# Second cross attention with its rounded projections in whole 16-bit numbers, output by token tile; peaks of the second self attention turned first

## What is computed

```python
def _qdq(x):
    s = jnp.maximum(jnp.max(jnp.abs(x), axis=-1, keepdims=True) / 127.0, 1e-08)
    return jnp.clip(jnp.round(x / s), -127.0, 127.0) * s
q = _qdq(x) @ _qdq(wq).T + bq
kv = cond @ wkv.T + bkv
k, v = jnp.split(kv, 2, axis=-1)
attn = jax.nn.softmax(jnp.einsum('bnhd,bmhd->bhnm', q, k) * scale, axis=-1)
o = jnp.einsum('bhnm,bmhd->bnhd', attn, v).reshape(B, N, C)
out = _qdq(o) @ _qdq(wp).T + bp
```

## Time and profile before

| | before |
|---|---|
| median of 3 runs | 1515.16 us |
| lowest and highest | 1513.21 and 1516.91 us |
| profiled execution, whole time | 1516.96 us |
| its span in the trace | 1515.1 us |
| TensorE busy, mean granted clock | 93%, 0.957 |
| VectorE, ScalarE, GpSimd busy | 66%, 52%, 5% |

### The profile page before, as it was taken

The page is one execution under the profiler, slowest core; times in us unless marked ns, Lnnn a source line. Parts: engine busy times, 40 slices in busy tenths (PEclk is TensorE's granted clock), DMA queues, the critical chain, the costliest instruction groups (busy, mean ns, idle before and its releaser), DMA issues. The chain is left out here.

```text
span 1515.1 us, 31884 instructions
## 1 busy us (share of the span) xinstructions
PE 1415.0 (93%) x11772; PEld 1087.6 (72%) x11772; DVE 999.5 (66%) x1651; ACT 783.7 (52%) x1130; POOL 78.4 (5%) x71
## 2 busy tenths in 40 slices
PE   6999999999979989999989999969999688899998
PEld 4677776777735479999977877846666365799997
DVE  6666677666645467666538777768999333676664
ACT  3677777777741545554422222327887103555552
POOL 0000000000010300000011121110000100000000
PEclk9999999999989979999999999978999769899999
DMA  5333443333223077656115233237785120676662
GB/s 167 73 89 86 121 104 85 83 83 89 49 76 141 1 244 264 206 197 209 37 47 168 106 126 109 84 87 164 170 175 116 49 53 9 207 254 211 213 216 75
DMA packets 133457, 190.94 MB, mean 126 GB/s; under 512 B 74972, under 2 KB 96702, under 8 KB 130175
## 3 DMA queue, kind: packets, MB, share of 16 engines
q1 hardware_dynamic: 133391, 190.04, 43.6%
HBM read 153.86 MB, written 17.48 MB: 113 GB/s over the span
## 5 line engine op out<-in xcount | busy, mean ns | idle before, releaser
L187 PE MATMUL psum<-m_x_hi,m_gu_hi 128*128 128x256 f32 x780 | 222.8, 286 | 3.2 <-DVE m_h L2381 2.9
L188 PE MATMUL psum<-m_x_hi,m_gu_lo 128*128 128x256 f32 x780 | 222.1, 285 | 0.0
L189 PE MATMUL psum<-m_x_lo,m_gu_hi 128*128 128x256 f32 x780 | 222.0, 285 | 0.0
L1527 DVE TENSOR_REDUCE x_peaks<-psum 128x2048 f32 (+1 forms) x64 | 146.4, 2291 | 51.6 <-PE psum L1419 51.6
L187 PE MATMUL psum<-x_w_hi,x_ctx_hi 128*128 128x256 f32 x512 | 159.0, 311 | 0.0
L187 PEld LDWEIGHTS psum<-m_x_hi,m_gu_hi 128*128 128x128 f32 x780 | 150.7, 193 | 6.9 <-DVE m_h L2381 3.3
L188 PEld LDWEIGHTS psum<-m_x_hi,m_gu_lo 128*128 128x128 f32 x780 | 150.7, 193 | 1.5
L189 PEld LDWEIGHTS psum<-m_x_lo,m_gu_hi 128*128 128x128 f32 x780 | 150.5, 193 | 0.0
L188 PE MATMUL psum<-x_w_hi,x_ctx_lo 128*128 128x256 f32 x512 | 145.1, 283 | 0.0
L189 PE MATMUL psum<-x_w_lo,x_ctx_hi 128*128 128x256 f32 x512 | 144.9, 283 | 0.0
L1657 DVE TENSOR_TENSOR e_wqp<-e_wqp,x_probs 128x1024 f32<-128x1024 f32 x124 | 141.7, 1220 | 3.1 <-ACT x_probs L1672 2.8
(11 more groups left out here) (310 smaller groups left out, 2777.9 us busy)
## 6 DMA issues: line engine op xcount, KB each, us to landing
m_gu_raw<-in_m_gu SPq DMA_DIRECT2D x41, 768.0 KB, 4.3
e_w<-x_keys_dram SPq DMA_DIRECT2D x45, 512.0 KB, 6.9
m_gu_raw<-in_m_gu SPq DMA_DIRECT2D x18, 1024.0 KB, 5.0
x_ctx_raw<-in_ctxT SPq DMA_DIRECT2D x64, 256.0 KB, 2.7
m_dn_raw<-in_m_down SPq DMA_DIRECT2D x16, 768.0 KB, 4.3
m_dn_raw<-in_m_down SPq DMA_DIRECT2D x18, 512.0 KB, 5.1
x_keys_dram<-x_keys_hi SPq DMA_DIRECT2D x16, 512.0 KB, 3.2
x_keys_dram<-e_wqp SPq DMA_DIRECT2D x16, 512.0 KB, 2.6
```

What stands on the lines that cost most here:

```text
L187: pe.matmul(out, a[0], b[0], start=start, stop=False, skip_group_check=True)
L188: pe.matmul(out, a[1], b[0], start=False, stop=False, skip_group_check=True)
L189: return pe.matmul(out, a[0], b[1], start=False, stop=stop, skip_group_check=True)
L1527: dve.tensor_reduce(peaks[:, t, 4 * m:4 * m + 4, bass.ds(k, 1)].rearrange("p h k -> p (h k)"), g.psum[:, at:at + BANKS, :], AX, ALU.max).t ...
```

## The change

- `grid_step` no longer multiplies by the step size in its last step. It writes the whole numbers (up to 127 in magnitude) to a tensor given as `whole`. `wqT`, `wpT`, the rounded x (`x16`) and the rounded output (`o16`) become 16-bit floats. The step sizes of the weights are kept in `g.x1_grid`.
- Query: ScalarE spreads the step size of each token over 128 columns, TensorE turns it into a row for all partitions (bank 3), and ScalarE copies that (`x_row`) before its half of x. VectorE then scales the product (`scalar_tensor_tensor`), and adds the bias in a further instruction.
- `c3`: ScalarE spreads the step sizes of wp (four instructions), TensorE turns them after the peaks, ScalarE copies them (`wp_row`), and only then fills its row of ones.
- `c4`: SyncE loads `bp` and `bv` (256 KB each) ahead of its loop; GpSimd adds `bp` to x in two instructions. The sums are no longer rotated.
- `c5`: the reciprocals are taken of the sums as they stand in PSUM, 512 per partition and tile, and outputs are divided straight from PSUM before they are turned. Each token tile goes alone through bias, rounding, turning, copy and product; then it is scaled and added. The product with one row of ones is gone.
- `stage_attn1`: the peaks are turned ahead of the values' product; `tops(0)` waits for the first half of the queries alone.

```diff
@@ grid_step
-            dve.tensor_scalar(tiles[i], tiles[i], ROUND, col(grid, i), ALU.subtract, ALU.mult).then_inc(done, 1)
+            dve.tensor_scalar(whole[i], tiles[i], ROUND, None, ALU.subtract).then_inc(done, 1)
@@ stage_cross1
-        wpT = sb("wpT", [P, NC, D], F32)
-        wqT = sb("wqT", [P, NC, D], F32)
+        wpT = sb("wpT", [P, NC, D], F16)
+        wqT = sb("wqT", [P, NC, D], F16)
@@ query on TensorE
-                        pe.wait_ge(x_rounded, 1)
+                        pe.wait_ge(x_spread_ready, NT)
+                        for t in range(NT):
+                            last = pe.transpose(g.bank[3][:, t * P:(t + 1) * P], x_spread[:, t, :], g.ident[:, :])
+                        last.then_inc(x_row_turned, 1)
+                        pe.wait_ge(grid_done, NT * GRID_STEPS[-1])
...
+                            if m == 2:
+                                pe.wait_ge(x_row_taken, 1)
@@ query on ScalarE
+                    act.wait_ge(grid_done, 2 * NT)
+                    for t in range(NT):
+                        act.activation(x_spread[:, t, :], g.zeros[:, 0:P], ACT.Identity,
+                                       bias=grid[:, t:t + 1]).then_inc(x_spread_ready, 1)
...
+                            act.wait_ge(x_row_turned, 1)
+                            act.activation(x_row[:, :], g.bank[3][:, 0:L], ACT.Copy).then_inc(x_row_taken, 1)
@@ query on VectorE
                         for m in range(NC):
+                            dve.scalar_tensor_tensor(out=qT[:, m, :],
+                                                     in0=g.bank[2 + m // 2][:, (m % 2) * L:(m % 2 + 1) * L],
+                                                     scalar=g.x1_grid[:, 0, m:m + 1], in1=x_row[:, :], op0=ALU.mult,
+                                                     op1=ALU.mult).then_inc(q_ready, 1)
+                        for m in range(NC):
+                            dve.tensor_scalar(qT[:, m, :], qT[:, m, :], bias[:, 0, m:m + 1], Y_HD ** -0.5, ALU.add,
+                                              ALU.mult).then_inc(q_ready, 1)
@@ c3 on ScalarE
+                    for m in range(NC):
+                        act.activation(wp_spread[:, m, :], g.zeros[:, 0:P], ACT.Identity,
+                                       bias=g.x1_grid[:, 1, m:m + 1]).then_inc(wp_spread_ready, 1)
+                    act.wait_ge(wp_row_turned, 1)
+                    act.activation(wp_row[:, :], g.bank[1][:, :], ACT.Copy)
@@ c4
+                    pool.wait_ge(bp_loaded, 16)
+                    for t in range(NT):
+                        pool.tensor_tensor(g.x[:, t, :], g.x[:, t, :], bp[:, :], ALU.add)
...
+                    sp.dma_start(bp[:, :], A["x1_bp"]).then_inc(bp_loaded, 16)
+                    sp.dma_start(bv[:, :], A["x1_bv"]).then_inc(bv_loaded, 16)
@@ c5 on TensorE
+                    for t in range(NT):
+                        pe.wait_ge(divided, t + 1)
+                        for grp in range(4):
+                            last = pe.transpose(g.bank[t][:, grp * P:(grp + 1) * P], oT[:, t, grp // 2, grp % 2, :],
+                                                g.ident[:, :])
                         last.then_inc(turned, 1)
                     for t in range(NT):
+                        pe.wait_ge(step_done, GRID_STEPS[-1] * (t + 1))
                         for c in range(NC):
+                            last = pe.transpose(g.bank[2 + t].bitcast(F16)[:, c * P:(c + 1) * P],
+                                                o16[:, t, c * P:(c + 1) * P], g.ident16[:, :])
+                        last.then_inc(o_turned, 1)
+                        pe.wait_ge(o_taken, t + 1)
+                        for c in range(NC):
+                            last = pe.matmul(g.bank[6 + t][:, :], oqT[:, t, c * P:(c + 1) * P], wpT[:, c, :],
+                                             start=(c == 0), stop=(c == NC - 1))
+                        last.then_inc(projected, 1)
@@ c5 on VectorE
                     for t in range(NT):
+                        dve.reciprocal(inv[:, t, :, :, :], of_tile(6, t)).then_inc(inverted, 1)
                         dve.wait_ge(inverted, t + 1)
+                        dve.tensor_tensor(oT[:, t, :, :, :], of_tile(4, t), inv[:, t, :, :, :],
+                                          ALU.mult).then_inc(divided, 1)
                     dve.wait_ge(bv_loaded, 16)
                     for t in range(NT):
+                        dve.wait_ge(turned, t + 1)
+                        dve.tensor_tensor(o[:, t, :], g.bank[t][:, :], bv[:, :], ALU.add).then_inc(biased, 1)
+                        dve.wait_ge(biased, t + 1)
+                        for step in range(len(GRID_STEPS)):
+                            grid_step(dve, step, [o[:, t, :]], [o16[:, t, :]], grid[:, t:t + 1], per_grid[:, t:t + 1],
+                                      step_done, GRID_STEPS[-1] * t)
                     for t in range(NT):
                         dve.wait_ge(projected, t + 1)
+                        dve.scalar_tensor_tensor(out=y[:, t, :], in0=g.bank[6 + t][:, :], scalar=grid[:, t:t + 1],
+                                                 in1=wp_row[:, :], op0=ALU.mult, op1=ALU.mult).then_inc(scaled, 1)
+                        dve.wait_ge(scaled, t + 1)
+                        residual(dve, g, t, y[:, t, :])
@@ stage_attn1 on TensorE
-                pe.wait_ge(q_taken, 2)
                 for i in range(B_KV):
+                    if i < 2:
+                        pe.wait_ge(q_taken, i + 1)
                     if i == B_KV // 2:
                         pe.wait_ge(q_placed, 16 * J)
                     tops(i)
+                pe.wait_ge(tops_read, B_KV)
+                for t in range(NT):
+                    last = pe.transpose(g.bank[2][0:B_H, t * P:(t + 1) * P], peak[:, t, :], g.ident[:, :])
+                last.then_inc(peak_turned, 1)
                 pe.wait_ge(wv_loaded, 16)
-                pe.wait_ge(tops_read, B_KV - 1)
```

136 lines of the change are left out of this document (52 added, 84 removed).

## The result

The kernel after takes 1500.07 us (median of 4 runs, 1498.84 to 1501.55) against 1516.04 us of the kernel before beside it (4 runs, 1513.21 to 1518.34): a ratio of 0.990, 95% interval 0.9884 to 0.9916, so 16 us or 1% less. The prediction was 1501.2 us, range 1496.0 to 1508.0; its sum was 14.0 us. The profiled execution took 1501.55 us, its span 1499.7.

The account below looks back on a forecast made before the run. Bounds: TensorE up to and in the chunk loop, VectorE in the context-tile loop, a chain of waits in the output block. 4.9 + 7.8 + 2.5 - 1.2 = 14.0 us saved; 1515.16 - 14.0 = 1501.2 us, range 1496.0 to 1508.0.

Parts of the forecast that it names:

- Query: Query's product: 16 records instead of 32 save 5.3 us, the row copy costs 0.4; net 4.9 saved, passed on whole.
- the longer idle brings the clock to 0.50: Query, lower end of the gain: after some 2.5 us idle, product and part of the keys cost about 2 us more.
- Peaks' block: Before the context-tile loop: block ends about 0.9 us later, hidden by the second scores' wait for keys; counted 0, bounds 0 to 0.9.
- GpSimd's sums: Loop over context tiles: adding bp on GpSimd disturbs VectorE's gapless additions; 1.2 us lost, middle of 0 and 2.4.
- Port rival: Context-tile loop: both GpSimd sums each stop VectorE for 1.2 us, 1.2 more than counted; 1502.4 us; chance 0.20.
- Output block: End of second cross attention: a chain of waits, by token tile with 16-bit products, ends at 1194.9 instead of 1202.7; 7.8 us saved.
- Self attention: Second self attention: peaks turned first bring transfers earlier and perhaps a higher clock; 2.5 us saved, bounds 0.7 and 4.1.
- The transfer's part: Second self attention: peaks turned earlier let their DMAs land 1.2 us sooner; gain 0.7 to 1.2, taken as 1.0.
- The clock's part: Second self attention: without the pause before the first score the clock may be 2.4 GHz; at most 2.9 us, half taken, 1.5.
- Clock rival: Query's idle brings 1.2 GHz (1.9 us lost) and the self attention's clock stays low (1.7 less gained); 1504.8 us; chance 0.17.
- The rival that has the kernel slower: TensorE, nearly idle in the output block, stays at 1.2 GHz through the self attention; 19 us lost, 1521.7 us; chance 0.03.
- 16-bit no faster: Query and output products gain no speed from 16 bits: query loses 0.4 us, output block gains about 3; 1511.3 us; chance 0.06.

Follow-up runs that it names:

- e10: Kernel after with GpSimd's two sums moved to the start of the loop over chunks and ScalarE's row of ones filled first; 1500.62 us, ratio 0.9888.
- e15: Kernel after with the second cross attention's output product in fp32 instead of 16 bits; 1507.54 us, ratio 0.9933.
- e1: Kernel before with only the second self attention's edit (peaks turned ahead of the values' product); 1514.68 us, ratio 0.999.
- e13: Kernel after with e3, e10, the query's copies reordered, and needless products in TensorE's waits from query to self attention; 1490.32 us, ratio 0.9849.
- e11: Kernel after with three needless fp32 products ahead of the second self attention's search for peaks; 1494.80 us, ratio 0.9855.
- e3: Kernel after with outputs and sums copied and turned before dividing, as before, so 16 reciprocals per tile instead of 512; 1494.37 us, ratio 0.9842.

## Why the prediction was right

**The total: right, with errors that cancelled.** The parts gave 1.5 us less than predicted in the query and 0.7 less in the peaks' block, and 1.3 more in the loop over context tiles, 0.3 more in the output block and 1.3 more in the self attention. That they add up to 15.0 for 14.0 is in part luck.

**Query: right but for the clock.** 16 records by 0.12 gave 1.9 us; the rows show 1.92 at full clock. Row copy 0.4: the product began 0.27 later. Net gain 5.0 in six of the nine kernels that have the new query and no warm products there, against the predicted 4.9; in the profile of after it was 3.4, because of "the longer idle brings the clock to 0.50", which the step had as its lower end ("about 2 us more"; measured 1.6). VectorE and the loop over chunks passed the gain on, as the step said.

**Peaks' block: the delay was right, the cover held for a reason that wasn't worked out.** The delay was put at 0.9, and it was 0.7 to 1.0 in nine kernels. The step then hid it behind the DMA wait at 1024.25. The first group of scores and the first exponential come ahead of that wait, and they were late. VectorE's first addition was not; it came 16.8 us after the peaks' reduction, against 17.2 in before. The second group's keys had landed 9.8 us after the reduction instead of 10.7, so it no longer waited for them and began 0.4 sooner. By e10 the order on ScalarE costs 0.4 us there, within the step's 0 to 0.9.

**GpSimd's sums: the number was near, the path to it was not.** The step said that "anything that holds VectorE up there reaches the end", and took 1.2 as the middle between 0 and 2.4, without a mechanism. The runs show 2.2 us lost where the two engines meet, 1.2 made good in the rest of the row, and about 1 at the end. The reading behind it, a row "without a gap", was too coarse: 25 additions in 28.65 us have small pauses between them. The Port rival had the loss at the spot right (2.2 of its 2.4) and the time wrong. The loop's total in after (151.05 against 151.13) hides the 1 us, since its first addition came 1.1 us sooner after the first exponential.

**Output block: 8.1 for 7.8.** Reciprocals 3.36 (predicted 3.4), tile 0 rounded 13.5 us after the first sum (13.7), four products at 1.2 GHz 1.86 (1.7 to 2.0), end at 21.45 (21.8). The chain ended on VectorE and TensorE in turn, as drawn. What the sum left open, e15 settles: the 16 bits are 5.9 of it. Sum and measurement both count from the profile of before, 29.55; from e1's 27.94 the gain would be 6.5.

**Self attention: right on average, by two ends that don't average in a run.** The transfer's part, predicted 1.0, is 0.7 to 1.2 in all eight kernels. The clock's part is 2.9 or about nothing, kept in four of eight; "half" describes no run, but their mean (2.2 together) is near the 2.5. In the profile of after it was the whole: 3.8.

**The rivals.** The Clock rival was half true in the profile of after: its query half came (1.6), its self-attention half did not. The rival that has the kernel slower, with a clock that never rises in the self attention, did not come; it overlooked that the peaks' search runs at 1.2 GHz already in before and can only gain there. "16-bit no faster" is excluded by 1.92 and 1.02 us.

**What is open.** Why the clock falls in some profiles and not in others with the same idle time ahead (query 3 of 9; second score 4 of 8). Each kernel's timeline is read from one profiled execution, so how often each case comes in the timed runs isn't known. The two groups of e13's runs, 7 us apart and with different mean clocks, may be this; no trace of the slower group shows where. What the order by token tile is worth by itself is open too.

## What to carry to other kernels

A product in 16 bits pays its full difference where TensorE is the chain: 5.0 and 5.9 us here, and both follow nearly from record counts and one neighbouring row. After every edit that makes TensorE's work shorter, look for the waits that it makes longer. And where a stage full of TensorE work runs at clock 0.50 behind a pause of 1.7 us, try needless products in the pause: three of them, 1.3 us of work, brought 5.8 us up to the first score and 4.4 over the stage. Read a row of back-to-back work for its spacing, and not only for gaps: here 0.01 us an addition made good 1.2 us. And when a forecast takes the middle between two ends, ask whether the runs will lie at the middle or at the ends: the range has to hold the ends.

## What the runs showed of the hardware

- The clock stayed at 1.2 GHz through 17 us of work on 16 rows with TensorE busy 17.52 of 18 us, and stayed at 2.4 GHz through the same work, busy 11.59 of 14 us, when the pause ahead was filled. What differed was the pause ahead of it: 1.69 us, and 0.44 us behind needless products (after and e11).
- A reciprocal on VectorE takes 3.36 us for 512 elements a partition and 0.26 for 16, from PSUM: 6.3 ns an element (after and e3).
- VectorE and GpSimd, both on operands in SBUF: an addition of 1024 up to 2.30 us instead of 1.22, a GpSimd sum of 512 2.28 instead of 1.28 (after, e10). In a row of 124 such additions, two sums took 2.2 us where they met it and 1.0 at its end.
